# Expert outputs weighed on VectorE after its sum, in a graph layer and mixture of experts kernel

## What is computed

```
x = x + gnn(layernorm(x), edges, W1_l, W1_r, b1, W2_l, W2_r, b2)   # x: 3125 x 256, 50000 edges
t = layernorm(x)
logits = t @ router_w.T                       # 8 experts
rw, re = top_k(softmax(logits), 2)            # two experts for each node
rw = rw / sum(rw)
out = t
for e in range(8):
    h = gelu(t @ w1[e] + b1[e])
    out = out + combine[:, e] * (h @ w2[e] + b2[e])
x = x + out
```

## Time and profile before

| | us |
|---|---|
| median of 3 runs | 641.64 |
| lowest and highest | 641.53, 642.04 |
| the profiled execution | 639.34 |
| its span, first to last instruction | 637.4 |
| busy in it: TensorE matmuls | 560.5 |
| VectorE | 350.4 |
| ScalarE | 222.8 |
| GpSimd | 181.1 |

### The profile page before, as it was taken

The page is one execution under the profiler, slowest core; times in us unless marked ns, Lnnn a source line. Parts: engine busy times, 40 slices in busy tenths (PEclk is TensorE's granted clock), DMA queues, the critical chain, the costliest instruction groups (busy, mean ns, idle before and its releaser), DMA issues.

```text
span 637.4 us, 11408 instructions
## 1 busy us (share of the span) xinstructions
PE 560.5 (88%) x3021; PEld 332.4 (52%) x3022; DVE 350.4 (55%) x1199; ACT 222.8 (35%) x422; POOL 181.1 (28%) x175
## 2 busy tenths in 40 slices
PE   5999999999999999998999999999603998797993
PEld 3445545555555555553545454454302777676772
DVE  5977666667666676643556657667770222212221
ACT  5667734444435444421010000000010544445452
POOL 4830000000000000000304253343460474765774
PEclk9999999999999999999999999999855999898998
DMA  8321200111111111127313365432274686787883
GB/s 271 119 66 59 84 28 31 50 50 50 36 40 51 50 44 32 51 51 229 94 58 101 118 191 153 156 126 85 74 213 108 149 176 145 138 167 143 179 171 57
DMA packets 70581, 66.84 MB, mean 105 GB/s; under 512 B 11989, under 2 KB 68676, under 8 KB 70542
## 3 DMA queue, kind: packets, MB, share of 16 engines
q1 hardware_dynamic: 55486, 50.61, 26.6%
q0 software_dynamic: 11456, 14.25, 12.1%
q10 hardware_dynamic: 3600, 1.48, 0.9%
HBM read 38.11 MB, written 29.14 MB: 106 GB/s over the span
## 4 chain that ended last, share of the span: by engine, by line
PE 46%; DMA 16%; issue 13%; DVE 12%; POOL 7%; POOLq 2%; ACT 1%; SPq 0%; DVEq 0%; ACTq 0%
PE bank L1243 21%; DMA out<-adj 11%; PE counts_ps L638 6%; PE bank L1233 6%; PE bank L1158 5%; PE counts_ps L1243 4%; POOL xs_dram L574 3%; POOL stat L567 2%; POOL out L611 2%; DMA y<-y_dram 1%; DMA xs_dram<-w,onehots 1%; PE counts_ps L1385 1%; DVE adj L1122 1%; DMA xs_dram<-onehots 1%; DMA y<-in_x 1%
## 5 line engine op out<-in xcount | busy, mean ns | idle before, releaser
L1243 PE MATMUL bank<-y,adj 128*128 128x512 f16 x625 | 154.7, 379 | 0.4 <-ACT zt L1451 0.4
L1243 PE MATMUL counts_ps<-y,adj 128*128 128x512 f16 x625 | 144.3, 379 | 2.1 <-DMA y<-y_dram 2.1
L611 POOL DMA_INDIRECT out<-adj x56 | 87.0, 1553 | 67.1 <-ACT adj L1580 36.1
L645 ACT ACTIVATE adj<-counts_ps 128x1000 f32 (+1 forms) x80 | 80.2, 1004 | 61.2 <-PE counts_ps L638 61.2
L1243 PEld LDWEIGHTS counts_ps<-y,adj 128*128 128x128 f16 x625 | 60.7, 101 | 64.9 <-DMA y<-y_dram 4.1
L1243 PEld LDWEIGHTS bank<-y,adj 128*128 128x128 f16 x625 | 57.8, 97 | 59.5 <-issue 13.7
L1385 PE MATMUL counts_ps<-adj 128*128 128x256 f32 x240 | 62.3, 405 | 14.8 <-ACT adj L1566 13.3
L555 POOL IOTA onehots<- 128x8 int32 x1 | 0.1, 143 | 231.5 <-PE counts_ps L638 231.5
L1385 PEld LDWEIGHTS counts_ps<-adj 128*128 128x128 f32 x240 | 46.1, 200 | 28.4 <-ACT adj L1566 18.9
L638 PEld LDWEIGHTS counts_ps<-onehots 125*128 125x128 f16 x640 | 41.1, 98 | 27.1 <-issue 10.8
L624 DVE TENSOR_TENSOR onehots<-iota,lo_t 125x1024 f16<-125x1024 f16 x80 | 54.5, 682 | 0.3 <-DVE rdeg L894 0.2
(11 more groups left out here) (230 smaller groups left out, 630.6 us busy)
## 6 DMA issues: line engine op xcount, KB each, us to landing
adj<-in_L_ffn_w SPq DMA_DIRECT2D x38, 256.0 KB, 3.4
adj<-xs_dram SPq DMA_DIRECT2D x31, 264.0 KB, 2.9
rows<-z_dram SPq DMA_DIRECT2D x49, 128.0 KB, 2.1
z_dram<-zt SPq DMA_DIRECT2D x36, 128.0 KB, 1.7
rows<-in_x SPq DMA_DIRECT2D x24, 128.0 KB
out<-yo SPq DMA_DIRECT2D x24, 128.0 KB
y_dram<-yo SPq DMA_DIRECT2D x23, 128.0 KB, 1.7
y<-y_dram SPq DMA_DIRECT2D x4, 640.0 KB, 6.6
```

Of the source, the lines that this page charges most:

```text
L611: g.indirect_dma_start(out, bass.IndirectOffsetOnAxis(ap=ids[s][:, h:h + 1], axis=0), ye[s][:, h, :], None, bounds_check=N - 1, oob_is_err ...
L645: nc.scalar.activation(adj[:, :, bass.ds(at, GW * WD)].rearrange("p b (h d) -> p b h d", d=WD), counts_ps[:, 2 * (group % 2):2 * (group % ...
L1243: last = te.matmul(to, adj[:, b, t * P:(t + 1) * P], y[:, b, :], start=(b == 0), stop=(b == NT - 1))
```

## The change

VectorE's `result` now waits for TensorE's product alone, forms ysum, and only then waits for the landing of pair i-2. It then copies the node numbers and multiplies each half of ysum by the weight column into `ye[s]` itself. ScalarE's `weigh` is gone; GpSimd's wait on `ye_in` loses the 4 that ScalarE had added to that semaphore ahead of the loop.

```diff
@@ gpsimd
-                        pool.wait_ge(S["ye_in"], n * 4 + (2 * s + h + 5))
+                        pool.wait_ge(S["ye_in"], n * 4 + (2 * s + h + 1))
@@ vector: result(i, n, s)
                 dve.wait_ge(S["meta_in"], n * 2 + (s + 1))
-                for h in range(2):
-                    dve.wait_ge(ye_out[s][h], n * 16 + 16)
-                v.tensor_copy(ids[s], tab_id[:, bass.ds(i * 2, 2)])
-                dve.wait_ge(S["ye_in"], n * 4 + (2 * s + 2))
                 dve.wait_ge(S["ye_ps"], n * 2 + (s + 1))
                 v.tensor_tensor(ysum[s], y_ps[s], ew(eb2_sb, e, 0).rearrange("p (h n) -> p h n", h=1)
                                 .to_broadcast((P, 2, D)), ALU.add).then_inc(S["ysum_in"], 1)
+                for h in range(2):
+                    dve.wait_ge(ye_out[s][h], n * 16 + 16)
+                    dve.sem_inc(S["held"], 1)
+                v.tensor_copy(ids[s], tab_id[:, bass.ds(i * 2, 2)])
+                dve.wait_ge(S["ysum_in"], n * 2 + (s + 3))
+                dve.sem_inc(S["held"], 1)
+                for h in range(2):
+                    v.tensor_scalar(ye[s][:, h, :], ysum[s][:, h, :], tab_c[:, bass.ds(i * 2 + h, 1)], None, ALU.mult
+                                    ).then_inc(S["ye_in"], 1)
@@ scalar
-            def weigh(i, n, s):
-                act.wait_ge(S["ysum_in"], i + 3)
-                for h in range(2):
-                    act.wait_ge(ye_out[s][h], n * 16 + 16)
-                    a.activation(ye[s][:, h, :], ysum[s][:, h, :], ACT.Copy, scale=tab_c[:, bass.ds(i * 2 + h, 1)]
-                                 ).then_inc(S["ye_in"], 1)
-
-            act.sem_inc(S["ye_in"], 4)
...
                     i = n * 2 + s
-                    weigh(i, n, s)
                     gelu(i + 2, s)
                     turn_rows(i + 3, 1 - s)
```

## The result

The changed kernel takes 637.82 us, the median of 6 runs (635.01 to 639.73), against 641.84 for the kernel before on the same chip: a ratio of 0.993 (0.9902 to 0.9958), 4.0 us. On a second chip it was 635.81 against 642.92, 0.9895 (0.9865 to 0.9925), 7.1 us. The forecast was a gain of 7.5 and a time of 634.1. Direction and range held; on the first chip half of the forecast gain came, on the second nearly all.

A forecast was written before the change was run, and what follows sets the result against it. The expert loop was taken as bound by a chain of output landings: twelve links by 0.9 is 10.8 us, 8.5 after floors and first link, less 1.0 for longer landings, gain 7.5, so 641.64 becomes 634.1; range 631 to 639.6.

The forecast's parts named there:

- What bounds the loop: Expert loop, 128.7 us: one chain through output landings, twelve links over two pairs (8.97 each) and three single links.
- Steps 1 to 3: Landing to GpSimd's next issue: ysum before the wait, weighing on VectorE, one more wait; 0.9 us off each two-pair link.
- The floors: GpSimd's 7.42 and TensorE's 7.8 us per two pairs take back 1.8 us, the first link's unhidden product 0.5.
- Landings: Output landings in the expert loop, with busier DMA engines: 15 landings by 0.07, 1.0 us taken back.
- rival C: Closer-packed DMAs lift mean landing from 4.13 to 4.9: 644.6 us, chance 0.06; milder no-change form 0.07.
- Step 4: ScalarE leaves the landing wait; TensorE's 13.3 us of waits go, but beside the landing chain, so nothing counted.
- Rival A: TensorE takes over as the expert loop's bound, its stalls using up the slack; 637.6 us; chance 0.13.
- Its sign: What would show Rival A: VectorE's ysum waiting for TensorE in most pairs.
- Rival B: VectorE's product is short (0.27 us) and holds GpSimd, putting off landings; 637.1 us; chance 0.12.

The follow-up runs named there:

- e11: e7 with rounds of four pairs and four buffers for ids and ye, so the landing waited for is pair i-4's: 625.04 us, 0.9756.
- e7: Changed kernel with SyncE's load of w1 for pair i+2 put ahead of the row load of pair i+3: 633.93 us, 0.9886.
- e8: Changed kernel with the landing wait put back ahead of ysum; VectorE still weighs: 644.0 us, 1.0051.
- e10: Kernel before the change with SyncE's w1 load put ahead of its row load: 636.67 us, 0.9936.
- e5: Changed kernel with the loop's w1 loads cut from 256 KB to 16 KB: 627.5 us, 0.9797.
- e6: Kernel before the change with the loop's w1 loads cut from 256 KB to 16 KB: 633.6 us, 0.9896.
- e2: Changed kernel with the product as a TENSOR_TENSOR against the broadcast weight column instead of a TENSOR_SCALAR: 639.53 us, 0.9929.
- e1: Changed kernel run again with no edit: 635.81 us, 0.9895.
- e3: Changed kernel, but ScalarE still waits for ysum and the landing of pair i-2 before GELU of pair i+2, without weighing: 637.42 us, 0.9929.
- e4: Kernel before the change with only ysum moved ahead of the landing wait; ScalarE still weighs: 637.49 us, 0.9919.

## Why the prediction was right, and where it was off

**What bounds the loop**: right. e11, which takes the two-pair links out, shortens the loop by 8 us against e7 and by 13.5 to 15 against before (there with the swap and the change in it).

**Steps 1 to 3, the link**: right, and a little small. From landing to issue 2.99 became 1.94; the forecast was 0.9, measured 1.05. The product took 0.35 (median; 0.37 in the mean) and not 0.41. The nearest row was of a TENSOR_SCALAR with two pointer scalars; this one has one.

**The floors**: 12 x 0.9 less 2.3 was 8.5; measured 7.1, of 12 x 1.05. What is missing to 12.6 are links in which the pair waited behind GpSimd's issues of the pair before or for TensorE, 5.5 and not 2.3. Behind pair 20 the pair before is often an even one, and the landings of pairs 20, 22 and 24 had grown from 3.75 to 4.08 before to 4.51 to 5.46, so a part of the 5.5 is landings too, and the 4.4 below is the least that they took.

**Landings, the term that was mis-sized**: I took 15 x 0.07 = 1.0, from the medians of a dense and a sparse stretch, and measured 4.4. The medians of the two stretches compared how dense they are, and density doesn't order the landings: at a DMA share of 0.79 over the loop they are 4.05 before and 4.40 in e8, at 0.80 they are 3.89 in e10, and at 0.86, the densest, 4.34 in e11. What does tell is how a load falls against a second half. So rival C had the effect right, at half its price (it decides from 0.57 a landing, and 0.3 came), and its reason, that a shorter loop packs the same bytes closer, is not borne out. That the loads have to do with it is shown by e5 and e6: without w1's bytes the change lengthens landings by 0.11 in the mean, and the four long ones that are left each have a row load within 1 us behind them.

**Step 4, "I count nothing"**: failed as written. I had said that SyncE's row loads want keep_meta two pairs later, and had not looked at what is queued behind them on SyncE: w1. TensorE's wait for w1 went from 1.3 to 12.7 us. Most of it lay beside the landing chain; in the stretch shown above it was on the path, and put off pair 18 by 2.0 us. In e7, without this queue, the link to pair 19 is 1.0 us shorter; what the queue costs in all isn't settled.

**Rival A** (TensorE takes over): not as the rule, at two places: pair 4, and pairs 18 and 19, in both executions of the changed kernel, were issued 0.9 to 2.0 us later than their landing asked for, behind a late ysum. Its sign, as I had written it, came all the same: ysum waited for TensorE 24 times of 28 (45.7 us). But ysum now stands ahead of the landing wait, so this wait is most often spent where the landing would have been waited for, and the sign told nothing.

**Rival B**: GpSimd was not held; its 1.55 stayed in the median, and landings are as long with the slow form (e2). What happened is the reverse. In the changed kernel five products took 0.50 to 0.69 us, and these are the five that began 0.47 to 0.65 us after the start of an indirect DMA of GpSimd; all of them ended 1.15 to 1.18 us after that start. It is the same in e1, e3, e7, e8 and e11: every product that began 0.47 to 0.70 us in took 0.45 us or more. One of them, in the row of two products that begins at 505.03 and takes 0.94:

```profile
504.53 1.59 POOL L611 DMA_INDIRECT out<-adj  x1 [0.30 <-issue]
505.03 0.94 DVE L1127 TENSOR_SCALAR adj<-adj 128x256 f32<-128x256 f32 x2 [0.18 <-issue]
```

In e2 four products of the other form, TENSOR_TENSOR, began in the same way 0.51 to 0.63 us in and took 0.42 to 0.43, like all others. So GpSimd's instruction holds the short form, by up to 0.34 us, and in all the 56 products lost some 1.1 us by it. The Trainium skill, "SBUF — State Buffer", section "SBUF: two separate sides", has such a lock: whichever of a VectorE operation in a two-port mode and a GpSimd operation starts first has the shared ports for its whole instruction, and the other waits. The trace agrees in who waits for whom, but the product ended 0.4 us before GpSimd's instruction did. The Trainium skill, "VectorE: DVE Perf Modes", section "The perf-mode tier table", gives the f32 TENSOR_SCALAR a double rate; 352 ns against 422 for the TENSOR_TENSOR of the same size agrees with a faster mode, though it lies between the 0.41 and the 0.27 that I had worked out for single and double rate.

**Luck**: on the first chip 637.8 is outside the stretch to which I gave a half (632.5 to 636.5), and nearest to the times of A and B (637.6, 637.1), neither of which happened; it is in the range because that was drawn past them. And errors of both signs met in the sum: the link gained more than I had counted (1.05 for 0.9), landings and the links' waits cost more.

**Open**: why the change moves the loads against the second halves as it does. e3, e4 and e8 each keep a part of the old kernel and all move the loads or lengthen landings; no run set the time of the loads by itself.

## What to carry to other kernels

Where a loop's path runs over DMA landings, work that needn't wait for the landing belongs ahead of the wait (here 1.05 us for each link), but more buffers, which take the landing off the path altogether, brought another 8 us (e11 against e7, by their ratios) where the whole change had brought 4 to 7. Before an engine is freed from a wait, look at what its wait paced, down to the second DMA in the queue behind it. The order of two loads on one queue is worth a run of its own: here 5 us for swapping them in the kernel before.

## What the hardware showed

An accumulating indirect DMA of 128 rows landed in 3.98 us in the mean with no w1 load of 256 KB issued within 1 us of it, in 4.54 with one, and in 5.00 with one and a row load of 264 KB within 2 us behind it. These are means over seven executions, sorted afterwards; in the first class the means of single executions go from 3.61 to 4.37. With the w1 loads cut to 16 KB (e5 and e6) those of the same pairs took 3.56 to 4.14, and 4.67 to 4.90 the four times that a row load was issued 0.91 to 0.98 us behind. GpSimd's own part had its median at 1.55 us throughout, and an f32 TENSOR_SCALAR that VectorE began 0.47 to 0.65 us into it took up to 0.34 us longer, a TENSOR_TENSOR did not.
